# A decoder layer on one core: attention's values one group later, a narrow last tile of keys, a table of exponentials loaded by hand

## What is computed

```python
v = (values @ Wv.T).reshape(N, -1, HEADS, HEAD_DIM)      # values = keys = the context, N = 8
k = (keys @ Wk.T).reshape(N, -1, HEADS, HEAD_DIM)        # 16 heads of 16 features
q = (query @ Wq.T).reshape(N, -1, HEADS, HEAD_DIM)
energy = jnp.einsum('nqhd,nkhd->nhqk', q, k)
attn = jax.nn.softmax(energy / HEAD_DIM ** 0.5, axis=-1)
out = jnp.einsum('nhqk,nkhd->nqhd', attn, v).reshape(N, Q, EMBED)
return out @ Wo.T + bo
```

## Time and profile before

| | |
|---|---|
| median of 3 runs | 1074.76 us (1073.32 to 1075.15) |
| the profiled execution | 1068.39 us, its span 1066.7 us |
| busy over the span | TensorE 970.4 us (91%), its weight loads 693.8 us, VectorE 888.6 us (83%), ScalarE 818.6 us (77%), GpSimd 686.3 us (64%) |
| mean clock granted to TensorE | 0.958 of full |
| chain that ended last | TensorE 54%, VectorE 26%, issue 11%, ScalarE 7% |

### The profile page before, as it was taken

How to read it: one execution, slowest core, us unless ns; L and a number is a source line. 1 busy time by engine, 2 the same in 40 slices (tenths; PEclk the granted TensorE clock), 3 DMA queues, 4 the chain that set the end, 5 groups by cost and what they waited for, 6 DMA issues and landing times.

```text
span 1066.7 us, 17481 instructions
## 1 busy us (share of the span) xinstructions
PE 970.4 (91%) x6032; PEld 693.8 (65%) x6032; DVE 888.6 (83%) x1027; ACT 818.6 (77%) x1802; POOL 686.3 (64%) x417
## 2 busy tenths in 40 slices
PE   5994898998999989999898999799988989999995
PEld 3542555655656656566565566577766779899995
DVE  6798999999999999999999997756677755466663
ACT  3999998998999999999999861456556665577773
POOL 2001899999999999999999993761111016244552
PEclk9996799999999999999999999979899979899999
DMA  6001344444444444434444432310000007999942
GB/s 197 9 8 39 100 111 112 111 114 110 111 112 108 112 111 112 113 108 112 112 112 111 113 88 68 117 38 16 15 2 2 2 1 255 361 367 361 361 122 51
DMA packets 86775, 122.22 MB, mean 115 GB/s; under 512 B 11127, under 2 KB 79984, under 8 KB 86672
## 3 DMA queue, kind: packets, MB, share of 16 engines
q1 hardware_dynamic: 82848, 115.78, 37.3%
q0 software_dynamic: 3840, 5.34, 2.5%
HBM read 115.92 MB, written 5.99 MB: 114 GB/s over the span
## 4 chain that ended last, share of the span: by engine, by line
PE 54%; DVE 26%; issue 11%; ACT 7%; DMA 1%; DVEq 0%; POOLq 0%; POOL 0%; ACTq 0%
DVE states L1925 15%; PE ps L1357 15%; PE ps L1249 10%; PE ps L1715 7%; PE ps L1232 5%; DVE states L1903 4%; PE ps L1337 4%; PE ps L1490 3%; PE ps L1502 2%; DVE neg_max L2041 2%; ACT probs L1119 2%; PE ps L1518 1%; PE ps L1345 1%; PE ps L1242 1%; PE ps L1537 1%
## 5 line engine op out<-in xcount | busy, mean ns | idle before, releaser
L760 POOL TENSOR_TENSOR states<-states,c_row 128x800 f32<-128x800 f32 x255 | 472.9, 1901 | 90.8 <-DVE states L1925 90.5
L1357 PE MATMUL ps<-states,ident 128*128 128x400 f32 x1024 | 382.0, 509 | 11.4 <-DVE u L1933 11.4
L1357 PEld LDWEIGHTS ps<-states,ident 128*128 128x128 f32 x1024 | 187.3, 193 | 117.2 <-DVE u L1933 12.7
L1925 DVE TENSOR_TENSOR_SCAN states<-sb_decay,ps 128x800 f32<-128x800 f32 x128 | 231.9, 1812 | 5.2 <-ACT sb_decay L1033 3.8
L1925 DVE TENSOR_TENSOR_SCAN states<-ps,states 128x800 f32<-128x800 f32 x128 | 230.2, 1798 | 1.1 <-ACT ps L1033 1.1
L1025 ACT ACTIVATE xT<-xn_tok,xT 100x256 f32<-100x256 f32 x512 | 216.5, 494 | 1.1 <-PE ps L1337 0.8
L1033 ACT ACTIVATE ps<-dt,neg_a 128x396 f32<-128x396 f32 x256 | 141.2, 583 | 45.1 <-DVE states L1925 44.2
L1337 PEld LDWEIGHTS ps<-ident,xT 100*128 100x128 f32 x1024 | 100.7, 145 | 82.1 <-issue 62.6
L1033 ACT ACTIVATE sb_decay<-dt,neg_a 128x396 f32<-128x396 f32 x256 | 144.4, 611 | 1.0 <-DVE states L1925 0.9
L1337 PE MATMUL ps<-ident,xT 100*128 100x100 f32 x1024 | 114.2, 256 | 30.2 <-DVE states L1925 17.6
L1119 ACT ACTIVATE probs<-ps,neg_max 100x361 f32<-100x361 f32 x128 | 70.9, 560 | 65.0 <-DVE neg_max L2041 64.5
(11 more groups left out here) (273 smaller groups left out, 1643.5 us busy)
## 6 DMA issues: line engine op xcount, KB each, us to landing
c_row<-rows SPq DMA_DIRECT2D x256, 200.0 KB, 3.1
w_tile<-in_w SPq DMA_DIRECT2D x40, 1024.0 KB, 10.9
b_row<-rows SPq DMA_DIRECT2D x32, 200.0 KB, 3.1
ctx<-in_ctxT SPq DMA_DIRECT2D x8, 361.0 KB, 3.4
win<-in_winT SPq DMA_DIRECT2D x2, 1024.0 KB, 10.9
shared_raw<-in_w SPq DMA_DIRECT2D x2, 1024.0 KB, 6.7
wout<-in_woutT SPq DMA_DIRECT2D x2, 512.0 KB, 6.7
token_rows<-rows_src SPq DMA_DIRECT2D x1, 828.1 KB
```

The lines of the kernel that those rows point to most:

```text
L760: nc.gpsimd.tensor_tensor(st, st, c_row[i % C_SLOTS][:].unsqueeze(1).broadcast_to([P, CP, TQ]), ALU.mult).then_inc(product_ready, 1)
L1357: mm = nc.tensor.matmul(ps[:, j, 0:TQ], ident[:], states[i % RING][:, j * TQ:(j + 1) * TQ], start=(n == 0), stop=(n == N - 1), skip_group_ ...
L1925: nc.vector.tensor_tensor_scan(st, rates, inflows, 0.0, ALU.mult, ALU.add).then_inc(scan_done, 1)
```

## The change

`VALUES_AT` goes from (5, 6) to (6, 7), on TensorE and on VectorE alike. `turn_probs` takes 105 columns of the third tile of keys instead of 128, and the memsets that zeroed the columns behind them go, with their semaphore. ScalarE loads the table that has the exponential by name before it waits for the first maximum.

```diff
--- before.py
+++ after.py
@@ -97,7 +97,7 @@
 PAR = QUAD // HD
 VW = 3 * HD
 HEAD_CONSTS = 5
-MASS_AT, PROJECT_AT, KEYS_AT, VALUES_AT = 1, 2, (3, 4), (5, 6)
+MASS_AT, PROJECT_AT, KEYS_AT, VALUES_AT = 1, 2, (3, 4), (6, 7)
 QUADS = P // QUAD
 
 FIRST_KEYS, FIRST_VALUES = (0, 1), (4, 5)
@@ -484,7 +484,6 @@
         mix_done = sem("mix_done")
         mix_copied = sem("mix_copied")
         y_gated = sem("y_gated")
-        probs_zeroed = sem("probs_zeroed")
         mask_ready = sem("mask_ready")
         v_zeroed = sem("v_zeroed")
         inv_rows_ready = sem("inv_rows_ready")
@@ -549,6 +548,9 @@
             par, j = divmod(rest, P // QUAD)
             return m, j, par
 
+        def key_tile(kt):
+            return slice(kt * P, min((kt + 1) * P, S))
+
         def group(b, g):
 
             return (b, b % 2, g) if g < GROUPS else (b + 1, (b + 1) % 2, g - GROUPS)
@@ -793,8 +795,6 @@
                     nc.gpsimd.memset(part[:, :, S:].bitcast(F32), 0.0).then_inc(kv_split, 1)
             for b in range(2):
                 split_context(b, b, 1)
-            for r in range(2):
-                nc.gpsimd.memset(probs[r][:, :, S:], 0.0).then_inc(probs_zeroed, 1)
             pool.wait_ge(xn_ready, (1 + DIRS + 1) * B)
             nc.gpsimd.tensor_tensor(x_tok[:], x_tok[:], bias_tok[:, 1:2, :].broadcast_to([L, B, D]), ALU.add
                                     ).then_inc(bias_added, 1)
@@ -1138,7 +1138,7 @@
 
             for m in range(KD):
                 high_keys(0, 0, m, FIRST_KEYS[m])
-            act.wait_ge(probs_zeroed, 2)
+            nc.scalar.preload_act_table_set("natural_log_exp_and_others")
             exponentials(0, 0, 0)
             exponentials(0, 0, 1)
             for m in range(KD):
@@ -1499,8 +1499,9 @@
                         pe.wait_ge(by, GROUPS * b + g)
                 for j in range(2):
                     for kt in range(KT):
-                        mm = nc.tensor.transpose(ps[:, 4 + j, kt * L:(kt + 1) * L], probs[g % 2][:, j, tile(kt)],
-                                                 ident[0:L, 0:L])
+                        cols = key_tile(kt)
+                        mm = nc.tensor.transpose(ps[0:cols.stop - cols.start, 4 + j, kt * L:(kt + 1) * L],
+                                                 probs[g % 2][:, j, cols], ident[0:L, 0:L])
                 mm.then_inc(probsT_ready, 1)
 
             def weigh_values(b, r, s):
```

## The result

The changed kernel takes 1082.92 us in the median of four runs (1081.75 to 1084.66). The kernel before, timed beside it, takes 1074.04 (four runs, 1072.44 to 1075.15). The ratio is 1.0085 with a 95% interval of 1.0065 to 1.0105: slower, by 8.9 us. That lies inside the range of the prediction, but 6 us above its value.

The account below looks back on a forecast made before the run. No engine was full in the attention stage; its loop was read as a ring of waits. Preload -0.35, zeroing 0, narrow transposes 0 and later values +2.15 gave +1.8 us, a median of 1076.6; range 1070.0 to 1085.5.

Parts of the forecast that it names:

- Preload: Ahead of the attention loop: table load moves into ScalarE's idle wait, first transposes come 0.35 us earlier, once.
- Zeroing: Memsets on GpSimd and ScalarE's wait for them: wait already long met, so removal gains zero.
- Narrow transposes: TensorE's transposes in each group: taken as zero, range -2.4 to +2.4 us; 105-column load read as 19 ns shorter.
- Where the steps land: Sequence 3, groups 5 to 7: group 6's transposes at 775.24, split 0.14 us before the inv_rows copies.
- The collision: VectorE's inv_rows copies meet ctx_h; second passes in the gap before ctx_l: +0.43 us in five sequences, 2.15 us.
- Rivals 1 and 2: At the inv_rows copies: second copy waits out ctx_l, 1084.8, chance 0.25; or VectorE precedes the split, 1070.9, chance 0.12.
- The step that failed: Group 5: TensorE's wait grows from 0.91 to 1.33 us and was said to cost nothing.
- rival 3: TensorE's clock around the values: two falls fewer, 1070.5, chance 0.10; two more, 1082.7, chance 0.06.
- rival 1: Second inv_rows copy loses the gap and waits out ctx_l: +2.09 us per sequence, 1084.8 us, chance 0.25.

Follow-up runs that it names:

- e10: Kernel before with only the narrow transposes and without the zeroing and its wait, no preload: 1074.21 us, ratio 1.0009.
- e3: Changed kernel plus eight products nobody reads in TensorE's group 5 wait: 1079.72 us, ratio 1.0067 to the kernel before.
- e4: Changed kernel with GpSimd's split also waiting for the inv_rows of the same turn: 1080.59 us, ratio 1.0054 to the kernel before.
- e5: Changed kernel with both the eight unread products in group 5 and GpSimd's split after inv_rows: 1069.48 us, ratio 0.9981 to the kernel before.
- e0: Kernel before, unchanged, run and profiled again as a control: 1070.67 us, ratio 0.9983.
- e6: Changed kernel with the values back in groups 5 and 6 and GpSimd's split after inv_rows: 1069.36 us, ratio 0.9975 to the kernel before.

## Why the prediction was right or wrong

- **Preload: right in size.** From the queries to the first transposes it was 5.81 us, now 5.43 (681.97 to 687.40): -0.38 against -0.35 (the prediction's own working, 688.13 - 687.76, gives 0.37). Only part of its cause was right: e10 has the gain without the preload.
- **Zeroing:** called nothing; e10 shows that the edits without the preload bring the compiler's own table load forward, most likely by taking out this wait. In the whole change the two overlap, so the sum was right.
- **Narrow transposes: right in size, wrong in its reading of the load.** From the first of six to the next product it is still 0.62 us (797.36 to 797.98), against 0.61. The 19 ns less that the values' loads show didn't carry over: here the narrow load is the longer one, 185 ns against 152 (e10). The loop doesn't show it. The Trainium skill, "TensorE: Matmul & The Clock Gate", section "Weight-path perf modes", gives the fast load to 128 weights that aren't FP32; by that these loads should lose nothing with fewer columns, and the trace differs.
- **Where the steps land: right until the clock.** The transposes of group 6 are at the predicted instant, the wait is 1.32 for 1.33, ctx_h comes 0.11 before the copy for 0.14.
- **The collision: right, mechanism and price.** The second copy went through the gap, and e3 measured 0.42 per sequence for 0.43 (21.87 - 21.46 = 0.41 and 21.92 - 21.49 = 0.43). Rivals 1 and 2 are out: no copy waited for ctx_l, none was ahead of ctx_h. The Trainium skill, "SBUF — State Buffer", section "SBUF: two separate sides", has who starts first take the ports; this trace agrees (the second copy at 808.81, ctx_l at 808.88), don't.
- **The step that failed** is the last sentence on group 5: "TensorE's wait in group 5 grows to 1.3 us and costs nothing". I had priced that wait as time, and as time it was free: the periods without a fall are 20.81 with it (e4) and 20.79 to 20.88 without it (e5). But behind four of six such waits the granted clock fell. The mechanism stood in rival 3, with a chance of 0.06 and two more falls at 3.05 us, 6.1 in all; there were four more at 1.5 us, 6.0. That these two come out alike is luck, and so is the range: the time lies in it only because rival 1, which didn't happen, had set its upper end.
- **What I could have read.** The sentence "nothing in one execution says which" gave up too early: e0 shows the same falls in a second execution. Before had one in the middle of its loop, behind waits of 0.68 and 0.41 us, though four other turns with the same two waits had none. Its TensorE timeline:

```profile
758.55 0.71 PE L1502 MATMUL ps<-ident,probs 100*128 100x100 f32 x6 [0.68 <-DVE probsT L2047]
...
760.95 1.18 PE L1502 MATMUL ps<-ident,probs 100*128 100x100 f32 x6 [0.41 <-ACT probsT L1126]
```

  So a loop in which the clock falls behind waits that short can lose it behind a longer one, and a wait of 1.3 us in each of six turns had to be priced as up to six falls.
- **The sum, redone.** The four periods grew by 95.05 - 88.92 = 6.13 us: 4 x 0.43 for the collision and 3 x 1.5 for three short falls, 6.2; the third period's long fall is in both kernels. Over the loop, 5 x 0.43 and 4 x 1.5 make 8.2 against 7.8 measured. The forecast of +1.8 lacked the 6 us of falls. The medians differ by 1.1 more than the loops, and the stretch before the loop (-1.0) and the tail, which the prediction didn't treat, can hold that.

## What to carry to other kernels

A wait that grows on TensorE has two prices: its time, which another engine may hide, and the clock that it may cost the work behind it; look at the granted clock of the same stretch in the trace before, and if it falls anywhere in the loop, put a fall in every turn into the range. Work moved in one engine's order moves what it releases on others: follow that release to whom it collides with there, since a collision can also be ordered away by one wait on an engine with slack, as e6 does. Judge such a change by its stage, not by the whole, when another stage has two forms that differ by more than the effect.

## What the runs showed of the hardware

- TensorE's clock fell after a wait of 1.32 us between short products. It did so in unbroken work behind the wait, for 3.4 us, behind four of six such waits; which ones isn't explained. With eight products in the wait (1.21 us busy) it stayed at 2.4 GHz behind all six (e3).
- The falls had lengths of 3.4, 6.8, 10.2, 13.6 and 17.1 us or near them, and the two profiled executions of the kernel before had them at the same places; the mean clocks of its other runs, 0.951 to 0.958 over the whole span, say that not all have the same. A fall of 3.4 us cost 1.5 (23.40 - 21.87), one of 6.8 cost 3.0 to 3.1 (24.54 - 21.46 in before, 24.95 - 21.87 in e3, 23.77 - 20.81 in e4).
- Two inv_rows copies that come just behind the start of GpSimd's ctx_h take 1.43 to 1.50 us instead of 0.36, and 1.03 where they come while ctx_l is under way. Of two back to back, the second got through a gap of 0.07 us between GpSimd's instructions in each of five sequences.
- The weight load of a float32 transpose took longer with 105 columns (185 ns in e10) than with 128 (152), while the values' loads took 170 against 189.
- The scatters of the experts were on the chain in the long form of the tail, at first 7 to 10 us each, later 4 to 8; the long form is 5 to 12 us longer than the short one between the kernels profiled. Why one or the other comes stays open.
